# Rotary attention: short fp32 scores in three parts, rounded copies a step later, one pair of projections a step sooner

## The reference, cut to what matters

```python
def _L1_attn_ref(x, wq, wk, wv, wo):          # x: layer norm of (8, 1024, 256), hd = 128
    q = jnp.einsum('bsd,hd->bsh', x, wq)
    k = jnp.einsum('bsd,hd->bsh', x, wk)
    v = jnp.einsum('bsd,hd->bsh', x, wv)
    ...
    q = apply_rope(q)
    k = apply_rope(k)
    w = jax.nn.softmax(jnp.einsum('bqh,bkh->bqk', q, k) / scale, axis=-1)
    out = jnp.einsum('bqk,bkh->bqh', w, v)
    return jnp.einsum('bsh,dh->bsd', out, wo)
```

## Time and profile before

| | us |
|---|---|
| median of three runs | 4145.33 (4141.72 to 4146.5) |
| the profiled execution | 4151.7 |
| its span, first to last instruction | 4150.0 |
| the rotary attention, from its first transposes to its last output projection | about 431 (2397.3 to 2829) |
| TensorE busy there, 2450 to 2800 | 341.54 of 350 |

### The profile page before, as it was taken

How to read it: one execution, slowest core, us unless ns; L and a number is a source line. 1 busy time by engine, 2 the same in 40 slices (tenths; PEclk the granted TensorE clock), 3 DMA queues, 4 the chain that set the end, 5 groups by cost and what they waited for, 6 DMA issues and landing times. The chain is left out here.

```text
span 4150.0 us, 65963 instructions
## 1 busy us (share of the span) xinstructions
PE 3930.1 (95%) x23476; PEld 2360.4 (57%) x23476; DVE 2798.7 (67%) x5635; ACT 2639.6 (64%) x3262; POOL 1556.3 (38%) x1303
## 2 busy tenths in 40 slices
PE   7999999999969999999999989997999999999999
PEld 4555545555457787887878855554444444444444
DVE  7978888888578878788787555444545555554553
ACT  2666666666765545455454334444888888888888
POOL 3222222222334445344353221111555455555545
PEclk8999999999979999999999999998999999999999
DMA  7543544444132232322323210005676766667674
GB/s 180 127 105 85 114 100 101 107 92 116 43 119 61 83 101 62 109 75 81 103 61 106 63 35 1 1 1 121 143 163 145 165 152 154 154 146 160 150 160 100
DMA packets 205762, 430.00 MB, mean 104 GB/s; under 512 B 47584, under 2 KB 72560, under 8 KB 189056
## 3 DMA queue, kind: packets, MB, share of 16 engines
q1 hardware_dynamic: 193360, 411.56, 41.0%
q0 software_dynamic: 4160, 6.35, 0.7%
q10 hardware_dynamic: 7920, 7.87, 0.6%
HBM read 338.59 MB, written 87.03 MB: 103 GB/s over the span
## 5 line engine op out<-in xcount | busy, mean ns | idle before, releaser
L2254 ACT ACTIVATE gelu_out<-hidden,b_col 128x1024 f32<-128x1024 f32 x1024 | 1054.5, 1117 | 182.9 <-PE hidden L2177 177.5
L2237 POOL TENSOR_TENSOR combined<-combined,gated 128x512 f32<-128x512 f32 x480 | 621.3, 1294 | 648.9 <-DVE gated L2354 473.2
L715 DVE TENSOR_REDUCE maxima<-front_and_scoresT 128x1 f32<-128x512 f32 (+3 forms) x1280 | 725.9, 630 | 79.5 <-PE front_and_scoresT L517 49.8
L615 ACT ACTIVATE probsT<-front_and_scoresT 128x1024 f32<-128x1024 f32 (+3 forms) x768 | 596.6, 811 | 263.7 <-PE front_and_scoresT L550 258.4
L1179 POOL TENSOR_TENSOR pair_sums<-sims 128x1024 f32<-128x1024 f32 x256 | 482.9, 1902 | 662.6 <-DVEq L1311 412.3
L2354 DVE SCALAR_TENSOR_TENSOR gated<-out_bank,b_col,gates_spread 128x512 f32<-128x512 f32 x480 | 360.3, 751 | 512.3 <-PE out_bank L2185 483.6
L2177 PE MATMUL hidden<-slice_stack,w_stack 128*128 128x512 f32 x2048 | 623.2, 428 | 37.9 <-ACT gelu_out L2254 37.8
L1107 PE MATMUL dense<-xnT,dense_weights 128*128 128x512 f32 x2304 | 537.3, 395 | 12.5 <-ACT silu_down L1213 8.6
L2177 PEld LDWEIGHTS hidden<-slice_stack,w_stack 128*128 128x128 f32 x2048 | 354.9, 190 | 327.0 <-ACT gelu_out L2254 249.6
L2185 PE MATMUL out_bank<-gelu_out,w_sb 128*32 128x512 f32 x4096 | 517.1, 607 | 3.2 <-DVE combined L2354 3.0
L1107 PEld LDWEIGHTS dense<-xnT,dense_weights 128*128 128x128 f32 x2304 | 434.9, 189 | 112.9 <-ACT silu_down L1213 9.2
(11 more groups left out here) (202 smaller groups left out, 5069.2 us busy)
## 6 DMA issues: line engine op xcount, KB each, us to landing
gates_spread<-gate_scratch SPq DMA_DIRECT2D x512, 256.0 KB, 5.4
dense_weights<-dense_scratch SPq DMA_DIRECT2D x384, 256.0 KB, 2.8
stack_scratch<-split_parts SPq DMA_DIRECT2D x192, 256.0 KB, 3.1
slice_stack<-slice_scratch SPq DMA_DIRECT2D x128, 256.0 KB, 8.1
q_stack<-stack_scratch SPq DMA_DIRECT2D x64, 384.0 KB, 6.2
k_stack<-stack_scratch SPq DMA_DIRECT2D x64, 384.0 KB, 9.2
slice_scratch<-slice_parts SPq DMA_DIRECT2D x32, 512.0 KB, 5.6
out_x<-x_tiles ACTq DMA_DIRECT2D x15, 512.0 KB, 2.9
```

The costliest lines, as they stand in the source:

```text
L615: nc.scalar.activation(PT[:, i % NPT, 2 * pr:2 * pr + 2, at:BANK], R[:, low:high + 1:high - low, at:BANK], ACT.Exp, scale=SCALE).then_inc( ...
L715: nc.vector.tensor_reduce(dst, bank(k)[:, 0:parts * w].rearrange("p (a k) -> p a k", a=parts), AX.X, ALU.max)\
L2237: nc.gpsimd.tensor_tensor(CM[:, par, hc, :], CM[:, par, hc, :], Y[:, u % 2, :], ALU.add)\
L2254: nc.scalar.activation(GH[:, k % GHB, :, :], HP[k % HPB][:, :, :], ACT.Gelu, bias=b1c[:, n % E:n % E + 1])\
```

## The change

In `rotary_attention` `QK` is doubled and becomes F32R. A rotated half is no longer written by POOL in one go: POOL adds in place into `RC`, ACT writes a rounded copy of `RC` to `QK[:, 0]` (`high_part`), and POOL subtracts that copy from `RC` into `QK[:, 1]`. Each of the two score products becomes three short ones: rounded q with rounded k, rounded q with the rest of k, the rest of q with rounded k. ACT makes the rounded copies of a step's k and q at the end of the next step, behind `keep_turned`; at the opening each stands right behind its `swap`. k1 and q1 move from step 6 to step 5. To make room, `W1` is loaded in two halves of 8 experts into the space of the raw attention weights, and split at steps 20 and 30; SP waits for the turned weights before it begins.

```diff
-    SPLIT_AT = 20
+    SPLIT_AT = 20, 30
     FRONT_AT = {0: [("x", 0), ("x", 1)], 2: [("k", 0), ("q", 0)], 3: [("v", 0)],
-                4: [("x", 2), ("x", 3)], 6: [("k", 1), ("q", 1)], 7: [("v", 1)]}
+                4: [("x", 2), ("x", 3)], 5: [("k", 1), ("q", 1)], 7: [("v", 1)]}
...
+    PARTS = ((0, 0), (0, 1), (1, 0))
...
-        QK = sb("turned_qk", [HD, 2, 2, T])
+        QK = sb("turned_qk", [HD, 2, 2, 2, T], F32R)
...
-        W1R = sb("w1_raw", [P, later.E, later.I])
+        W1R = RAW[:, :, :].rearrange("p a d -> p (a d)").rearrange("p (e i) -> p e i", i=later.I)
...
+            sp.wait_ge(w_ready, 4)
             later.load(sp, W1R)
+            later.load_half(sp, W1R, 1)
...
-                    mm = nc.tensor.matmul(SC[n % 2][:, q * BANK:(q + 1) * BANK], QK[:, 0, b % 2, t * P:(t + 1) * P],
-                                          QK[:, 1, b % 2, q * BANK:(q + 1) * BANK], start=True, stop=True)
+                    for j, (of_q, of_k) in enumerate(PARTS):
+                        mm = nc.tensor.matmul(SC[n % 2][:, q * BANK:(q + 1) * BANK],
+                                              QK[:, of_q, 0, b % 2, t * P:(t + 1) * P],
+                                              QK[:, of_k, 1, b % 2, q * BANK:(q + 1) * BANK], start=(j == 0), stop=(j == 2))
...
-                nc.gpsimd.tensor_tensor(QK[:, SIDES.index(kind), b % 2, tok], RC[:, n % 2, :], SW[:, n % 2, :], ALU.add)\
+                nc.gpsimd.tensor_tensor(RC[:, n % 2, :], RC[:, n % 2, :], SW[:, n % 2, :], ALU.add).then_inc(rope_summed, 1)
+                pool.wait_ge(rope_high, n)
+                nc.gpsimd.tensor_tensor(QK[:, 1, SIDES.index(kind), b % 2, tok], RC[:, n % 2, :],
+                                        QK[:, 0, SIDES.index(kind), b % 2, tok].bitcast(F32), ALU.subtract)\
                   .then_inc(rope_ready, 1)
...
+            def high_part(kind, b, i):
+                n = r_count(kind, b, i)
+                act.wait_ge(rope_summed, n)
+                nc.scalar.activation(QK[:, 0, SIDES.index(kind), b % 2, i * BANK:(i + 1) * BANK], RC[:, n % 2, :], ACT.Copy)\
+                   .then_inc(rope_high, 1)
...
-            for kind, i in FRONT_FIRST:
-                if kind in SIDES:
-                    swap(kind, 0, i)
+            for k, i in R_ORDER:
+                swap(k, 0, i)
+                high_part(k, 0, i)
...
                 for unit in turn_units(n):
                     keep_turned(unit)
+                for unit in front_units(n - 1) if n else ():
+                    if unit[0] in SIDES:
+                        high_part(*unit)
...
-                if n == SPLIT_AT:
-                    later.split(dve, W1R)
+                if n in SPLIT_AT:
+                    later.split(dve, W1R, SPLIT_AT.index(n))
```

More of the change, by code:

```diff
@@ L1561, in rotary_attention @@
         sin_ready = sem("sin1_ready")
+        rope_summed = sem("rope1_summed")
+        rope_high = sem("rope1_high")
         rope_ready = sem("rope1_ready")
@@ L1921, in __init__ @@
         self.weights_in = ctx.enter_context(nc.semaphore("weights2_in"))
+        self.half_in = [ctx.enter_context(nc.semaphore(f"w1_half{k}_in")) for k in range(2)]
+        self.half_split = ctx.enter_context(nc.semaphore("w1_half_split"))
         self.rounded = ctx.enter_context(nc.semaphore("w1_rounded"))
@@ L1936, in load @@
             row = slice(self.HD * j, self.HD * (j + 1))
-            moves += [(raw[row, :, :], W1.rearrange("e d i -> d e i")), (self.b2c[row, :], b2.rearrange("e o -> o e")),
-                      (self.embd[row, j, :], emb)]
+            moves += [(self.b2c[row, :], b2.rearrange("e o -> o e")), (self.embd[row, j, :], emb)]
         self.all_in = 16 * len(moves)
@@ L1942, in load, with load_half, split @@
             sp.dma_start(dst, src, allow_slow_non_contiguous=True).then_inc(self.weights_in, 16)
-    def split(self, dve, raw):
-        low = slice(2 * self.HD, 4 * self.HD)
[L1947 to L1950, removed]
+        self.load_half(sp, raw, 0)
+    def load_half(self, sp, raw, k):
+        wait(sp, self.half_split, k)
+        experts = slice(k * self.E // 2, (k + 1) * self.E // 2)
+        for j in range(self.G):
+            sp.dma_start(raw[self.HD * j:self.HD * (j + 1), :, :], self.arrays[3][experts].rearrange("e d i -> d e i"),
+                         allow_slow_non_contiguous=True).then_inc(self.half_in[k], 16)
+    def split(self, dve, raw, k):
+        low = slice(2 * self.HD, 4 * self.HD)
+        if k == 0:
+            dve.wait_ge(self.weights_in, self.all_in)
+        dve.wait_ge(self.half_in[k], 16 * self.G)
+        part = self.w1s[:, k * self.E // 2:(k + 1) * self.E // 2, :]
+        self.nc.vector.tensor_copy(part, raw[:, :, :]).then_inc(self.rounded, 1)
+        dve.wait_ge(self.rounded, k + 1)
+        self.nc.vector.tensor_tensor(part[low], raw[low, :, :], part[low].bitcast(F32), ALU.subtract)\
+            .then_inc(self.half_split, 1)
 def mixture_ffn(nc, X, STATS, MEAN, RS, B, weights, out, ident):
```

## The result

The changed kernel takes 4155.49 us (median of 19 runs, 4144.82 to 4165.32), the one before 4145.33 us (median of 19 runs, 4136.9 to 4150.4). The ratio is 1.002, with a 95% interval of 1.0013 to 1.0028: slower by 10 us, 0.2%. The forecast was 4154, with slower (0.49) just ahead of the same (0.42). The profiled execution of the changed kernel has a span of 4163.6 us.

A forecast was written before the change was run, and what follows sets the result against it. The prediction took TensorE's list to bound the stage; -21.8 + 1.7 + 6.4 + 22.4 = +8.7 us gave a span of about 4158.7, put on the median as 4154 us, range 4140 to 4167.

The forecast's parts named there:

- Part 1: Scores: six short products replace four records, 0.34 us less a step, -21.8 us; +1.7 waited for in the last batch.
- the row of 144: Profile evidence for the score products: 144 short products in a row took 33.06 us, 0.230 each.
- Part 2: Opening: k0 and q0 ready at 2420.6, k1 at 2425.3 instead of 2418.9, +6.4 us.
- Part 3: Mid-stage hand-over: ACT held 5.2 us for POOL, TensorE waits 3.2 us in each of 7 batches, +22.4 us.
- Part 4: Hidden work: input norms meeting POOL end some 2 us later; W1 splits and loads counted as 0.
- the old wait: TensorE's known wait of 0.6 to 0.7 us behind the first input pair, counted as kept.
- the rival that counted on it: Norms not delayed, wait behind the first input pair swallowed: 7 times 0.7, -5 us, 4149; 24%.
- The hidden hand-over: Mid-stage: ACT's copies come before their banks are wanted, the 22.4 us fall away, about 4132; 9%.
- The falling clock: Waits behind step 7 drop TensorE's clock, 1.7 us each at seven places, 4158 to 4166; 22%.
- the last rival: Scores: six products take 0.43 us each, +55 in place of -21.8, about 4230; 2%.

The follow-up runs named there:

- the short products alone: Kernel before with each fp32 score product made three short ones of rounded operands, without copies, subtractions or moved steps: 4128.01 us, ratio 0.9957.
- POOL in pairs: Changed kernel, but mid-stage POOL multiplies and adds both k and q before subtracting either: 4138.05 us, ratio 0.9978 to the kernel before.
- the form that does not contend: Changed kernel with input norms in the form that also writes a sum (unused; norms not right): 4160.47 us, ratio 1.004.

## Why the prediction was right

It was right by its own steps, most of them close. By the same division as the table, forecast and measured: up to the scores of step 8 +5.1 (6.4 at the opening, 1.4 of waits, less 2.7) and +5.1; the six later batches +2.9 and +6.7; from there to the end +0.8 and -1.0. Of the 3.8 us too little in the middle the splits of `W1` are 3.3. The sum is near in part because this and the 1.8 us too much at the end go against each other. The scores of the first and the last step lie 7.2 us further apart than before, where about 3 were forecast.

**Part 1** (-21.8, +1.7 given back in the last batch). The six scores take their bank for 1.39 us. In the trace they look longer:

```profile
2571.70 1.64 PE L1677 MATMUL scores<-turned_qk 128*128 128x512 f32 x6
2573.18 1.95 PE L1657 MATMUL ring<-w_turned,xnT 128*128 128x128 f32 x16
```

2571.70 to 2573.18 is 1.48, not 1.38. But the first of six is recorded 28 ns behind the last transpose, not 109 as before, so 0.08 of the 1.48 belongs to the transpose. The step saves 0.325 us, 20.8 in all, where 0.34 and 21.8 were forecast. The last batch takes 51.0 us and took 52.0. With the short products alone it takes 50.0: so it gives back 0.6 of its 2.6, and not the 1.7 that were forecast, and the hand-over at its start costs 1.0 and not 1.8. The cost is in its first two steps, 13.9 us against 12.9 with the short products alone. TensorE waits there for the exponential, which stands behind the rounded copies on ACT:

```profile
2788.74 1.64 PE L1677 MATMUL scores<-turned_qk 128*128 128x512 f32 x6
2791.94 1.06 PE L1687 MATMUL ring<-ident,probs 128*128 128x128 f32 x8 [1.56 <-ACT probs L1777]
```

A part of this wait comes off the one of the next product with the values, 0.49 us here and 1.26 with the short products alone. The two misses, 1.1 and 0.8, are the 1.8 us too much at the end. The Trainium skill (TensorE: Matmul & The Clock Gate, Wait — 56ns, not 53.3ns?) gives 215.7 ns, by which the saving would be larger; inside the six, behind the first two, the distances are 228 to 236 ns, so the trace does not agree with it and decides, as the row of 144 did.

**Part 2** (+6.4). The scores start at 2420.54 and 2425.12, forecast 2420.6 and 2425.3:

```profile
2420.54 1.65 PE L1677 MATMUL scores<-turned_qk 128*128 128x512 f32 x3 [6.28 <-POOL turned_qk L1744]
...
2425.12 1.65 PE L1677 MATMUL scores<-turned_qk 128*128 128x512 f32 x3 [2.94 <-POOL turned_qk L1744]
```

The half clock was met in both, but for 3.4 us before and for 10.2 now. TensorE was busy for 5.6 of the 10.2. From the second half of these scores to the scores of step 1 it took 5.22 us before and takes 5.24 now, so the longer stretch cost the saving of one step and no more.

**Part 3** (+22.4). Behind step 7 the chain is where it was said to be, in the timeline of ACT and TensorE:

```profile
2571.70 1.64 PE L1677 MATMUL scores<-turned_qk 128*128 128x512 f32 x6
...
2572.48 0.62 ACT L1771 ACTIVATE turned_qk<-rot_cos_part 128x512 fp32r<-128x512 f32 x1
...
2577.08 0.63 ACT L1771 ACTIVATE turned_qk<-rot_cos_part 128x512 fp32r<-128x512 f32 x1 [3.98 <-POOL rot_cos_part L1742]
...
2578.71 1.07 ACT L1786 ACTIVATE probsT<-ring 128x512 f32<-128x512 f32 x2
...
2579.35 0.65 PE L1638 MATMUL ring<-ident,xn 128*128 128x128 f32 x4 [1.06 <-ACT probsT L1786]
```

From the scores of step 7 at 2571.70 the first rounded copy begins at +0.8, the second at +5.4, the copies of the turned tile at +7.0, and the second input pair starts at +7.65. The forecast had +0.7, +5.3, +7.0 and +7.6. A later batch is 0.57 us longer than before; with 2.6 saved, the waits added 3.2 us a batch, the forecast's figure. Step 8 and its like are 1.37 us longer, 1.70 with their saving, where 1.8 was forecast. The wait itself is not as forecast: 1.06 us ahead of the second input pair and not 1.7, since TensorE begins the first pair at +5.97 and not at +5.4, 0.28 of it in a wait for the first norm. The wait ahead of q1 is 0.9 to 1.2 us, forecast 1.1 to 1.2, and the one for the bank of the first `y` 0.2, as forecast.

**Part 4.** The norms are held by POOL, four taking 3.43 us where they take 1.4 beside an idle POOL. Not all four are over 1 us, as was said: two are 1.43 and two 0.40. They end 2.0 us later, as forecast, and this keeps the old wait: the form that does not contend gave 0.7 us a batch, the figure of the rival that counted on it. Mis-sized was the split of `W1`, taken as 0 with a bound of 2: its second place cost 3.0 us in the changed kernel (55.49 against 52.5) and 4.1 with POOL in pairs. It stood beside POOL's work, its wait was long enough to lose clock, and neither was priced. The first place, step 20, cost 0.3.

**The rivals.** The hidden hand-over did not come, since ACT is held 5.2 us and not 3.5; POOL in pairs made it come, and the stage fell by 16.6 us. The falling clock came once, behind the split, and not behind the 1.8 us of each batch, which were seen at a granted clock of 1.00. The six products take 0.23 us each and not 0.43, and the last rival falls.

## What to carry to other kernels

When a value passes from one engine to another and back, and each engine's list is in order, look at what stands behind the wait on both: here a wait of POOL for the first half kept it from preparing the second, ACT stood for the second, and TensorE, two engines further on, waited for banks. Put all that can be prepared ahead of the first wait; this order alone was worth 16.6 us in the stage, nearly the 17.9 that the short products save by themselves. And before taking work off the engine that bounds a stage, follow its short steps by hand: it is there that a hold of 5 us comes through, while a share of busy time says that the other engines have room.

## What the runs showed of the hardware

- A TENSOR_TENSOR of DVE with both inputs in SBUF and one of POOL lengthen each other: 2.18 us for 64x1024, where the same instruction took 1.22 with POOL idle (the split at step 33), and 2.13 for POOL's 128x512, where 1.27 is usual. Which of the two stood for how long at which point was not measured by itself.
- The clock held at 1.00 over the waits of each batch, 1.2 us the longest of those by ACT; behind the wait of 3.57 us it was 0.50 for 3.41 us; with POOL in pairs and k1 and q1 in step 6, waits of up to 2.5 us, it was 0.98 in the mean; and in the changed kernel with k1 and q1 in step 6, with waits of up to 3.5 and 4.5 us, it was 0.94 in the mean.
- The first short product behind transposes is recorded 28 ns behind the last one, where an fp32 product stands 109 ns behind; the next follows at 316 ns instead of 231. Only the sum can be compared.
